# A time-mixing block cut into sixteen 256-token chunks and woven into the attention loop of a Perceiver layer

## The chip, the cores and the metric

The kernel runs on one core of one Trainium2 chip. The metric is the device time of one execution in microseconds. The core has five instruction streams that run side by side and meet only at semaphores: TensorE (PE, matmuls; its weight loads are shown as PEld), VectorE (DVE), ScalarE (ACT), GpSimd (POOL) and SyncE (SP, which here only issues DMAs).

## The reference

A layer over x (128 sequences of 32 tokens, 128 channels: 4096 tokens) and a context (128 x 257 x 96). Three blocks follow each other, each behind a layer norm with a residual; in a cut form:

```python
x = x + cross_attention(layernorm(x), ctx)        # 16 heads of 64, softmax over 257 context rows
x = x + time_mix(layernorm(x))                    # per sequence
x = x + ffn(layernorm(x))                         # each token through one of 8 experts (argmax)

# time_mix:
x_prev = x shifted by one token inside its sequence (zero first)
k, v = (x*mix_k + x_prev*(1-mix_k)) @ W_key.T, (x*mix_v + x_prev*(1-mix_v)) @ W_value.T
r = sigmoid((x*mix_r + x_prev*(1-mix_r)) @ W_receptance.T)
f_a = exp(k)*v / w**(t+1);  f_b = sum_of_head(exp(k)) / w**(t+1)       # w = exp(-exp(time_decay))
state_a, state_b = w**t * exclusive_cumsum(f_a), w**t * exclusive_cumsum(f_b)   # inf and nan become 0
wkv = (state_a + exp(time_first)*exp(k)*v) / max(state_b + exp(time_first)*sum_of_head(exp(k)), 1e-6)
out = (r * wkv) @ W_output.T
```

The shift and the running sums stay inside a sequence of 32 tokens, so the block can be cut at any sequence.

## The kernel before, in words

The tokens lie as 32 tiles ("groups", g) of 128 tokens, which are 4 sequences each. All tiles of x stay in SBUF in `R` (its first 128 columns are `X`), and each block adds its output there.

**Attention** is a software pipeline over the 128 sequences. One step handles one sequence in several stages at once, and each engine has its own copy of the step (`pe_step`, `act_step`, `dve_step`, `pool_step`). `where(it, j)` numbers them: an iteration of the hardware loop has eight steps, j = -1 to 6, and covers two groups. In a step, in this order:

- PE: transposes the context of sequence n+2 (`pe_ctxT`, L360), computes the scores of n+1 in tiles 0, 1 and 2 (`pe_scores`, L371), the queries of n+5 into bank 3 (`pe_q`, L383), and score tile 3, which uses bank 0 again and so waits for the exponential of tile 0 (`s_exp`). Then come probabilities times context (`pe_pv`, L394 and L400), once per group the output product (`pe_y`, L408, in steps 1 and 5), a small transpose that VectorE waits for (L449), and the transposes of the probabilities in two halves (`pe_probsT`, L416).
- DVE: copies the context (`cT`, L535), takes four row maxima (`nmax`, L511) with the low halves of Th between them (`Tl`, L507), then `ql` (L491), `rsum` (L518), `L12` (L522, printed as L), once per group the residual add (L526), and `Ol` (L530).
- ACT: `Th` (L462), four exponentials `Pe` (L468) with `qh` (L486) among them, and `Oh` (L477).
- POOL: `Pn` (L559, the probabilities times 1/sum, 128 x 1028), four small operations, and the split of the raw context in `chi` (L541) and `clo` (L545).

**Time mixing** follows in a pipeline of its own, `over_pairs`, over eight chunks (s) of 512 tokens. In a chunk DVE normalizes and clips, adds up and divides: `xn` (L656), `scl` (L1205), `sst` (L1209), `ekv` (L1216), `den` and `num` (L1219, L1221), `den` again (L1225), the reciprocal `rec` (L1228) and the running sums `cs` as one scan per sequence and sum (L1234, 32 per chunk). PE does five matmuls in fp32, ACT seven activations and POOL eight elementwise operations. Most tiles of this stage have two buffers.

**The expert block** follows: a third layer norm (`dve_var`, `dve_rstd`), routing, weight preparation and a loop over sorted tiles.

The order on each engine is the order of the code. Nothing is reordered by a scheduler, and an instruction that waits holds up all that stands behind it on its engine.

## Time and profile before

| | us |
|---|---|
| median of 3 runs (lowest, highest) | 1127.61 (1126.6, 1131.02) |
| the profiled execution's own time | 1121.37 |
| its span | 1119.7 |
| busy PE / DVE / ACT / POOL in the span | 921.9 / 856.5 / 665.6 / 634.8 |

The profile's page gives the busy time of each engine over the whole span, and the views behind it cut this by stretch. By the timeline the attention pipeline runs from about 43 us to 744 us, time mixing from there to 912 us, and the expert block to the end. Busy times are sums of instruction durations; PE's overlap, so that a PE that is busy all the time isn't by that alone at its limit, and successive instructions of DVE overlap by some 0.08 us.

### The profile page before, as it was taken

What the parts mean: (1) busy time and instruction counts of PE and PEld (TensorE: products, weight loads), DVE (VectorE), ACT (ScalarE), POOL (GpSimd) and SP (SyncE); (2) the same over time, 40 slices, a digit from 0 to 9 for tenths busy, and PEclk for the clock granted to TensorE, in tenths of its full rate; (3) what the DMA queues carried; (4) which work ended last, traced back from release to release, by engine and by line L of the source; (5) the groups of instructions that cost most, each with busy time, mean ns of one, the idle gap of its engine ahead of it and who ended that gap; (6) DMA issues with size and microseconds to landing.
All of it is one profiled execution on the core that took longest, in us unless ns stands there. A gap on an engine that the chain in (4) does not pass through costs nothing.

```text
span 1119.7 us, 30693 instructions
## 1 busy us (share of the span) xinstructions
PE 921.9 (82%) x9018; PEld 759.3 (68%) x9019; DVE 856.5 (76%) x2288; ACT 665.6 (59%) x1892; POOL 634.8 (57%) x983
## 2 busy tenths in 40 slices
PE   3899999999999999999999999965444436148885
PEld 3788888888888888888888888742222236136664
DVE  5888878878888887888888788757999976225543
ACT  2677767777776776777777677643121202136664
POOL 4466666665666666566566666626575510735453
PEclk9899999999999999999999999987676655659888
DMA  6100010010000001001000100039000000111110
GB/s 176 25 16 17 16 28 14 14 29 14 14 20 23 14 15 29 14 14 28 15 14 15 29 14 15 3 72 195 0 1 0 0 0 3 53 46 48 42 44 17
DMA packets 46488, 32.13 MB, mean 29 GB/s; under 512 B 6518, under 2 KB 44065, under 8 KB 46448
## 3 DMA queue, kind: packets, MB, share of 16 engines
q1 hardware_dynamic: 44144, 27.38, 10.0%
q0 software_dynamic: 2304, 4.25, 1.1%
q8 instruction: 20, 0.33, 0.1%
q14 instruction: 20, 0.16, 0.0%
HBM read 24.62 MB, written 7.52 MB: 29 GB/s over the span
## 4 chain that ended last, share of the span: by engine, by line
PE 72%; DVE 13%; issue 9%; ACT 3%; DMA 1%; POOL 1%; SPq 1%; ACTq 0%; DVEq 0%; POOLq 0%
PE bank L371 15%; PE bank L394 15%; PE bank L416 10%; PE bank L408 8%; PE bank L383 7%; DVE cs L1234 4%; PE bank L1114 4%; PE bank L1129 3%; PE bank L400 3%; PE bank L360 2%; DVE xn L656 1%; PE bank L663 1%; PE bank L1084 1%; DVE den L1225 1%; DMA wo_r<-in_L_xattn_Wo_dram 1%
## 5 line engine op out<-in xcount | busy, mean ns | idle before, releaser
L559 POOL TENSOR_TENSOR Pn<-Pe,rsum 128x1028 f32<-128x1028 f32 x128 | 243.1, 1899 | 226.6 <-DVE rsum L518 142.3
L468 ACT ACTIVATE Pe<-bank,nmax 128x257 f32<-128x257 f32 x512 | 239.5, 471 | 92.5 <-DVE nmax L511 92.4
L511 DVE TENSOR_REDUCE nmax<-bank 128x1 f32<-128x257 f32 x512 | 199.2, 409 | 1.2 <-PE bank L371 1.2
L371 PE MATMUL bank<-cT,qh 96*128 96x257 f16 x1024 | 185.2, 275 | 5.1 <-ACT Pe L468 4.1
L462 ACT ACTIVATE Th<-bank 128x512 f16<-128x512 f32 x256 | 138.9, 595 | 78.9 <-PE bank L416 78.9
L507 DVE TENSOR_TENSOR Tl<-bank,Th 128x512 f16<-128x512 f32 x256 | 172.8, 676 | 0.0
L371 PE MATMUL bank<-cT,ql 96*128 96x257 f16 x512 | 139.1, 272 | 0.0
L416 PE MATMUL bank<-identf,Pn 128*128 128x128 f32 x1024 | 133.5, 273 | 0.0
L416 PEld LDWEIGHTS bank<-identf,Pn 128*128 128x128 f32 x1024 | 109.8, 141 | 0.0
L491 DVE TENSOR_TENSOR ql<-bank,qh 96x512 f16<-96x512 f32 x128 | 87.9, 687 | 23.5 <-ACT qh L486 23.5
L468 ACT ACTIVATION_READ_ACCUMULATOR Pe<-bank,nmax 128x1 f32 x512 | 99.9, 195 | 0.0
L530 DVE TENSOR_TENSOR Ol<-bank,Oh 96x512 f16<-96x512 f32 x128 | 87.6, 685 | 12.4 <-ACT Oh L477 4.5
L371 PEld LDWEIGHTS bank<-cT,qh 96*128 96x128 f16 x1024 | 83.7, 97 | 18.8 <-issue 5.4
L383 PE MATMUL bank<-x1h,Ahi 128*96 (+1 forms) x512 | 93.5, 221 | 0.0
L383 PE MATMUL bank<-x1h,Alo 128*96 (+1 forms) x512 | 93.3, 220 | 0.0
L383 PE MATMUL bank<-x1l,Ahi 128*96 (+1 forms) x512 | 93.2, 220 | 0.0
L408 PE MATMUL bank<-Bhi,Oh 96*128 96x128 f16 x512 | 87.5, 219 | 1.5 <-DVE Ol L530 1.5
L408 PE MATMUL bank<-Bhi,Ol 96*128 96x128 f16 x512 | 87.4, 219 | 0.0
L408 PE MATMUL bank<-Blo,Oh 96*128 96x128 f16 x512 | 87.3, 219 | 0.0
L522 DVE COPY L<-bank 128x128 f16<-128x128 f16 x128 | 25.5, 200 | 73.1 <-PE bank L449 73.1
L477 ACT ACTIVATE Oh<-bank 96x512 f16<-96x512 f32 x128 | 75.8, 592 | 4.2 <-PE bank L400 3.2
L394 PE MATMUL bank<-Th,chi 128*96 128x512 f16 x256 | 76.6, 379 | 0.9 <-DVE Ol L530 0.9
(221 smaller groups left out, 2478.1 us busy)
## 6 DMA issues: line engine op xcount, KB each, us to landing
raw<-in_ctx_dram SPq DMA_DIRECT2D x32, 384.0 KB, 3.3
sorted_rows<-fill SPq DMA_DIRECT2D x1, 2620.0 KB, 20.8
xs<-sorted_rows SPq DMA_DIRECT2D x40, 65.5 KB, 1.8
R<-in_x_dram SPq DMA_DIRECT2D x4, 512.0 KB, 5.9
Z<-last_rows SPq DMA_DIRECT2D x128, 2.2 KB
w1r<-in_L_ffn_W_dram SPq DMA_DIRECT2D x8, 256.0 KB, 6.0
w2fr<-in_L_ffn_W_dram SPq DMA_DIRECT2D x8, 256.0 KB, 6.3
out_dram<-yout,idx POOLq DMA_INDIRECT x40, 2.3
```

The source lines that it names most:

```text
L371: last = nc.tensor.matmul(bank[SB[t]][:, 0:M], w[:, par, b, t * P:(t + 1) * P], cT[:, s4, c, 0:M], start=(k == 0), stop=(k == 2))
L383: last = nc.tensor.matmul(bank[b][0:CC, hh * P:(hh + 1) * P], w[:, h, :], a[:, tok], start=(k == 0), stop=(k == 2))
L394: nc.tensor.matmul(bank[6][0:CC, :], w[:, s8, c, :], p[:, par, c, :], start=(k == 0), stop=False)
L408: last = nc.tensor.matmul(bank[7][:, 512 - C:512], o[:, gp, h, :], w[:, h, :], start=(h == 0 and k == 0), stop=(h == H - 1 and k == 2))
L416: last = nc.tensor.transpose(bank[4 + c][:, t * P:(t + 1) * P], Pn[:, par, t, c * P:(c + 1) * P], identf[:, :])
L462: nc.scalar.activation(Th[:, n_par(j - 1), c, :], bank[4 + c][:, :], ACT.Copy).then_inc(s_Th, 1)
L468: nc.scalar.activation(Pe[:, n_par(j + 1), t, :], bank[SB[t]][:, 0:M], ACT.Exp, bias=nmax[:, n_par(j + 1), t:t + 1], accum_out=sums[:, n_p ...
L491: nc.vector.tensor_tensor(q_view(ql, par, c), bank[b][0:CC, :].rearrange("p (h b t) -> p h b t", h=QT, b=GB), q_view(qh, par, c), ALU.subt ...
L507: nc.vector.tensor_tensor(Tl[:, n_par(j - 1), t, :], bank[4 + t][:, :], Th[:, n_par(j - 1), t, :], ALU.subtract).then_inc(s_Tl, 1)
L511: nc.vector.tensor_reduce(nmax[:, n_par(j + 1), t:t + 1], bank[SB[t]][:, 0:M], AX.X, ALU.max, negate=True).then_inc(s_nmax, 1)
L530: nc.vector.tensor_tensor(Ol[sl], bank[6][0:CC, :].rearrange("p (h t) -> p h t", h=H), Oh[sl], ALU.subtract).then_inc(s_Ol, 1)
L559: nc.gpsimd.tensor_tensor(Pn[:, par, :, :], Pe[:, par, :, :], rsum[:, par, :].unsqueeze(2).broadcast_to([P, QT, M]), ALU.mult)\
```

## The change

The time-mixing block is cut into 16 chunks (c) of 256 tokens, two groups each. It no longer has a stage of its own: `pe_mix`, `act_mix`, `dve_mix` and `pool_mix` are called at the end of each step of the attention pipeline, and do the part of a chunk that the step number j names. Chunk c starts in iteration c+1, two iterations behind attention's start on its groups, and ends in iteration c+3. What is left after the last sequence is run down by `drain_mix`, in which the same steps go on without attention. The tiles of the stage have one buffer each and no longer share memory with attention's. The second layer norm's statistics are taken per group in the loop (bn_stats and bn_aggr on DVE), and its inverse root and the normalization are done on POOL (`pow` and a Newton step). The third layer norm's bn_stats are taken in the loop as well. The loads of the mixing weights, their transposes and the decay tables are needed ahead of the attention pipeline now. All of the block's matmuls go through bank 3, which `pe_q` also uses, so they stand at the end of a step, between the two halves of `pe_probsT`.

```diff
+    MG = 2
+    MT = MG * P
+    MCH = G // MG
...
                 wait(nc.tensor, s_pn, n + 1)
-                pe_probsT(n, n_par(j))
+                pe_probsT(n, n_par(j), 0)
+            pe_mix(it, j, n)
+            if exists(n):
+                pe_probsT(n, n_par(j), 1)
...
+            if j == 5 and chunk(it, 1) is not None:
+                c = it - 1
+                pe_mix_bank(it, j, n)
+                wait(nc.tensor, s_m["xc"], c + 1)
+                nc.tensor.matmul(bank[3][:, 0:MT], wka[:, :], xT33[:, :, 1:N + 1], start=True, stop=False)
+                nc.tensor.matmul(bank[3][:, 0:MT], wkb[:, :], xT33[:, :, 0:N], start=False, stop=True)\
+                    .then_inc(s_m["k"], 1)
...
+            if j == 5 and chunk(it, 1) is not None:
+                c = it - 1
+                wait(nc.scalar, s_m["ekv"], c)
+                wait(nc.scalar, s_m["k"], c + 1)
+                nc.scalar.activation(ek[:, :], bank[3][:, 0:MT], ACT.Exp).then_inc(s_m["ek"], 1)
+                wait(nc.scalar, s_m["xm"], 2 * c)
+                wait(nc.scalar, s_m["dx"], c + 1)
+                for k in range(2):
+                    last = nc.scalar.activation(mdx[:, k, :], dx[:, :], ACT.Copy, scale=mix[:, 1 + k:2 + k])
+                last.then_inc(s_m["mdx"], 1)
...
+            if j in (1, 2) and chunk(it, 2) is not None:
+                c, k = it - 2, j - 1
+                wait(nc.vector, s_m["st"], 2 * c)
+                wait(nc.vector, s_m["fab"], 2 * c + k + 1)
+                for b in range(MS):
+                    last = nc.vector.tensor_tensor_scan(cs[:, k, b, 1:N + 1], onesn[:, :], fab[:, k, b * N:(b + 1) * N],
+                                                        0.0, ALU.mult, ALU.add)
+                last.then_inc(s_m["cs"], 1)
...
+            if j == 3 and chunk(it, 2) is not None:
+                c = it - 2
+                wait(nc.vector, s_m["sst"], 2 * c)
+                for k in range(2):
+                    wait(nc.vector, s_m["st"], 2 * c + k + 1)
+                    nc.vector.tensor_scalar(scl[:, k, :], sraw[:, k, :], -FMAX, FMAX, ALU.max, ALU.min)\
+                        .then_inc(s_m["scl"], 1)
...
+            if j == 5 and chunk(it, 2) is not None:
+                c = it - 2
+                wait(nc.vector, s_m["o"], c)
+                wait(nc.vector, s_m["dm"], c + 1)
+                nc.vector.reciprocal(rec[:, :], denm[:, :]).then_inc(s_m["rec"], 1)
...
+        def drain_mix(step):
+            for j in range(2, 7):
+                step(LIT, j)
+            for j in range(-1, 7):
+                step(LIT + 1, j)
+            for j in range(-1, 3):
+                step(LIT + 2, j)
```

What `dve_mix` does in the other steps: j = -1 `ekv`; j = 1 the scans of the first sum and the residual add of chunk it-3; j = 2 two bn_stats of chunk it-3 and the scans of the second sum; j = 3 also `sst` twice; j = 4 `den`, `num`, `denm`. `pool_mix` does `fab` twice (j = 0), `sraw` (j = 1, 2), the normalization (j = 3, nine operations), `dx` (j = 5), `xm` twice and `oT` (j = 6). `pe_mix` has the transposes of xn (4), k (5), the head sums (6), v (-1), r (0) and the output (1). `act_mix` has the copy of xT (4), `ek` and `mdx` twice (5), `esum` (6), `er` and `er1` (0).

The order on VectorE from `rsum` to the first row maximum, in a step of the loop. Before:

```order
L518 RECIPROCAL rsum<-sums 128x4
L522 COPY L<-bank 128x128
L530 TENSOR_TENSOR Ol<-bank,Oh 96x16x32
L535 COPY cT<-bank 96x2x256
L23 REGISTER_ALU
L511 TENSOR_REDUCE nmax<-bank 128x1
```

The same place with the change, in step 4 (L is L12, er is er1):

```order
L638 RECIPROCAL rsum<-sums 128x4
L642 COPY L<-bank 128x128
L652 TENSOR_TENSOR Ol<-bank,Oh 96x16x32
L703 SCALAR_TENSOR_TENSOR den<-esum,nlw,sst 128x256
L706 SCALAR_TENSOR_TENSOR num<-ekv,nlw,sst 128x256
L711 SCALAR_TENSOR_TENSOR denm<-den,er 128x256
L721 COPY cT<-bank 96x2x256
```

Three operations with two SBUF tensors each now stand between `Ol` and the next step's `cT` and first maximum; in step 3 they are `scl` twice and `sst` twice.

The order on TensorE from the small transpose to the next step's context transposes. Before:

```order
L449 MATMUL bank<-ident,e12p 128x128 [waits s_elo,s_cT]
L416 MATMUL bank<-identf,Pn 128x128 [waits s_Tl,s_pn]
L416 MATMUL bank<-identf,Pn 128x128 x3
L416 MATMUL bank<-identf,Pn 128x128 [waits s_Tl]
L416 MATMUL bank<-identf,Pn 128x128 x3
L360 MATMUL bank<-ident,chi 96x128 [waits s_L12,s_cT,s_clo]
```

And now, in step -1:

```order
L465 MATMUL bank<-ident,e12p 128x128 [waits s_elo,s_cT]
L432 MATMUL bank<-identf,Pn 128x128 [waits s_Tl,s_pn]
L432 MATMUL bank<-identf,Pn 128x128 x3
L523 MATMUL bank<-xm,w2T 128x256 [waits m_xm,s_ql]
L432 MATMUL bank<-identf,Pn 128x128 [waits s_Tl]
L432 MATMUL bank<-identf,Pn 128x128 x3
L377 MATMUL bank<-ident,chi 96x128 [waits s_L12,s_cT,s_clo]
```

The mixing matmul stands between the halves of the probability transposes, and waits for `ql` of the same step as well as for its own input.

## Rows read from the trace of the kernel before

**Rows 1.** Busy us by stretch: PE, PEld, DVE, ACT, POOL, then PEclk and DMA.

```profile
110.00:440.00 330.00, 329.46 (x3592) 284.34 (x3590) 278.84 (x703) 248.59 (x734) 210.23 (x367) 1.00 0.07 18
800.00:900.00 100.00, 44.33 (x108) 24.32 (x108) 99.83 (x286) 19.17 (x32) 58.66 (x41) 0.66 0.00 0
```

**Rows 2.** Chain that ended last, two steps of attention: start, us, what.

```profile
399.96 2.68 PE bank L408 x48
402.64 0.06 PE bank L449
...
405.51 0.51 PE bank L371 x3
...
407.54 0.06 PE bank L449
...
412.26 0.06 PE bank L449
```

**Rows 3.** Timeline of all engines, score tile 3 of the first step.

```profile
404.89 0.48 ACT L468 ACTIVATE Pe<-bank,nmax 128x257 f32<-128x257 f32 x1 [0.63 <-DVE nmax L511]
...
405.50 0.11 PEld L371 LDWEIGHTS bank<-cT,qh 96*128 96x128 f16 x2 [0.18 <-ACT Pe L468]
```

**Rows 4.** Timeline of VectorE, 400 to 411 us.

```profile
402.74 0.23 DVE L522 COPY L<-bank 128x128 f16<-128x128 f16 x1 [2.31 <-PE bank L449]
...
407.83 0.16 DVE L518 RECIPROCAL rsum<-sums 128x4 f32<-128x4 f32 x1
...
408.20 0.69 DVE L530 TENSOR_TENSOR Ol<-bank,Oh 96x512 f16<-96x512 f32 x1
408.81 0.41 DVE L535 COPY cT<-bank 96x512 f16<-96x512 f16 x1
409.14 0.74 DVE L511 TENSOR_REDUCE nmax<-bank 128x1 f32<-128x257 f32 x2
```

**Rows 5.** Timeline of POOL in the same stretch.

```profile
400.58 1.90 POOL L559 TENSOR_TENSOR Pn<-Pe,rsum 128x1028 f32<-128x1028 f32 x1 [0.99 <-DVE rsum L518]
...
404.06 0.19 POOL L551 COPY cT<-c256T 96x2 f16 x1
408.16 1.90 POOL L559 TENSOR_TENSOR Pn<-Pe,rsum 128x1028 f32<-128x1028 f32 x1 [3.90 <-PE bank L416]
```

**Rows 6.** Timeline of VectorE in the time-mixing stage.

```profile
833.72 1.58 DVE L1225 SCALAR_TENSOR_TENSOR den<-den,er 128x512 f32<-128x512 f32 x1
...
882.03 1.49 DVE L1205 TENSOR_SCALAR scl<-sraw 128x512 f32<-128x512 f32 x2
...
899.34 0.76 DVE L1205 TENSOR_SCALAR scl<-sraw 128x512 f32<-128x512 f32 x2
...
902.66 0.68 DVE L1225 SCALAR_TENSOR_TENSOR den<-den,er 128x512 f32<-128x512 f32 x1
903.38 3.35 DVE L1228 RECIPROCAL rec<-den 128x512 f32<-128x512 f32 x1
```

**Rows 7.** Timeline of POOL in that stage.

```profile
833.21 1.55 POOL L828 TENSOR_TENSOR fab<-esum,iap 128x512 f32<-128x512 f32 x1
...
879.04 2.73 POOL L814 TENSOR_TENSOR sraw<-cs,apw 128x512 f32<-128x512 f32 x1 [1.62 <-DVE cs L1234]
```

**Rows 8.** Busy time of the scans of L1234 in one microsecond: DVE busy (instructions), PEclk.

```profile
893.80:894.80 1.00, 1.00 (x10) 0.50 0.00 0
```

**Rows 9.** Timeline of VectorE at both ends of the time-mixing stage.

```profile
744.03 0.29 DVE L526 TENSOR_TENSOR R<-R,bank 128x128 f32<-128x128 f32 x1 [3.02 <-PE bank L408]
...
912.08 0.22 DVE L630 TENSOR_TENSOR tmpv<-stats 128x32 f32<-128x32 f32 x1
```

**Rows 10.** Chain that ended last, a 512-wide fp32 matmul of the stage.

```profile
773.36 1.72 PE bank L1051 x2
```

**Rows 11.** Timeline of SyncE, the last issues ahead of the attention pipeline.

```profile
35.68 5.01 SPq L706 DMA_DIRECT2D dcy<-n_L_attn_time_first_dram  x8
```

**Rows 12.** Chain that ended last, TensorE's start into the attention pipeline.

```profile
43.63 0.41 PE bank L360 x4
```

More of the change, by code:

```diff
@@ L102, in perceiver_layer_kernel @@
         xn = sb("xn", [P, 2, CT, C])
+        stats2 = sb("stats2", [P, MG, 6])
+        mv = sb("mv", [P, MG, 2])
+        vep = sb("vep", [P, MG])
+        rs0 = sb("rs0", [P, MG])
+        rsq = sb("rsq", [P, MG])
+        rsv = sb("rsv", [P, MG])
+        rsc = sb("rsc", [P, MG])
+        rst2 = sb("rst2", [P, MG])
+        consts = sb("consts", [P, 3, MG])
+        xd = sb("xd", [P, MG, C])
+        xn2 = sb("xn2", [P, MG, C])
+        xT33 = sb("xT33", [P, MS, N + 1])
+        dx = sb("dx", [P, MT])
+        mdx = sb("mdx", [P, 2, MT])
+        xm = sb("xm", [P, 2, MT])
+        ek = sb("ek", [P, MT])
+        er = sb("er", [P, MT])
+        er1 = sb("er1", [P, MT])
+        esum = sb("esum", [P, MT])
+        ekv = sb("ekv", [P, MT])
+        fab = sb("fab", [P, 2, MT])
+        cs = sb("cs", [P, 2, MS, N + 1])
+        sraw = sb("sraw", [P, 2, MT])
+        scl = sb("scl", [P, 2, MT])
+        sst = sb("sst", [P, 2, MT])
+        num = sb("num", [P, MT])
+        den = sb("den", [P, MT])
+        denm = sb("denm", [P, MT])
+        rec = sb("rec", [P, MT])
+        oT = sb("oT", [P, MT])
         w2r = sb("w2r", [P, 4, C])
@@ L178, in perceiver_layer_kernel @@
         s_tdve = sem("s_tdve")
-        s_m = {n: sem("m_" + n) for n in ("w", "zero", "xn", "xT", "xc", "k", "v", "r", "ek", "er", "er1", "sum", "esum", "dx", "mdx", "xm",
-                                          "ekv", "fab", "cs", "st", "rec", "o", "y", "res", "ch")}
+        s_m = {n: sem("m_" + n) for n in ("w", "zero", "stat", "mv", "rs", "rs2", "xd", "xn", "xT", "xc", "k", "v", "r", "ek", "er", "er1", "sum",
+                                          "esum", "dx", "mdx", "xm", "ekv", "fab", "cs", "st", "scl", "sst", "dn", "num", "dm",
+                                          "rec", "o", "y", "res", "stat3")}
         s_w3 = sem("s_w3")
@@ L257, in lsb @@
             return late.enter_context(nc.sbuf_tensor(name, shape, dt))
-        xT33 = lsb("xT33", [P, 2, SEQ, N + 1])
-        dx = lsb("dx", [P, T])
-        mdx = lsb("mdx", [P, 2, T])
-        xm = lsb("xm", [P, 2, 2, T])
-        ek = lsb("ek", [P, 2, T])
-        er = lsb("er", [P, 2, T])
-        er1 = lsb("er1", [P, 2, T])
-        esum = lsb("esum", [P, 2, T])
-        ekv = lsb("ekv", [P, 2, T])
-        fab = lsb("fab", [P, 2, T])
-        cs = lsb("cs", [P, 2, SEQ, N + 1])
-        sraw = lsb("sraw", [P, 2, T])
-        scl = lsb("scl", [P, 2, T])
-        sst = lsb("sst", [P, 2, T])
-        num = lsb("num", [P, 2, T])
-        den = lsb("den", [P, T])
-        rec = lsb("rec", [P, 2, T])
-        oT = lsb("oT", [P, T])
         w1r = lsb("w1r", [P, E, FC, C])
@@ L576, in pipeline @@
+        LIT = B // 8
         def pipeline(eng, step):
-            for j in range(-1, 7):
-                step(0, j)
-            with eng.Fori(1, B // 8 - 1) as it:
+            for i in range(3):
+                for j in range(-1, 7):
+                    step(i, j)
+            with eng.Fori(3, LIT - 1) as it:
                 for j in range(-1, 7):
                     step(it, j)
-            for j in range(-1, 10):
-                step(B // 8 - 1, j)
+            for j in range(-1, 7):
+                step(LIT - 1, j)
+            for j in range(-1, 2):
+                step(LIT, j)
@@ L585, in time @@
+        def drain_mix(step):
+            for j in range(2, 7):
+                step(LIT, j)
+            for j in range(-1, 7):
+                step(LIT + 1, j)
+            for j in range(-1, 3):
+                step(LIT + 2, j)
         def time(a):
@@ L589, in over_seqs @@
         def over_seqs(a):
[L590 to L602 removed]
+            return a.unsqueeze(1).broadcast_to([P, MS, N])
         def over_tiles(eng, step, routed=True):
@@ L1238, in _ @@
-            over_pairs(dve_mix)(dve)
-            dve.wait_ge(s_m["res"], CH)
-            dve_var(chain, 2 * LS + 2)
-            dve_rstd(chain, 3)
             nc.vector.tensor_copy(R[:, :, C + 1], mean[:, :]).then_inc(s_row, 1)
```

430 lines of the change are left out of this document (233 added, 197 removed).

## The prediction

> **What bounds the kernel now.** I read the busy time by stretch first [rows 1]. Attention keeps PE busy for 329.46 of 330 us, but DVE is busy for 278.84 too, while time mixing, between 800 and 900 us, keeps DVE busy for 99.83 of 100 and PE for 44.33. So a stage limited by DVE is to be laid over one in which DVE has 15% left. Whether the left part can be used is a question of where it lies, and for that I read the chain and the timelines.
>
> The chain through attention lies on PE alone: an ordinary step takes 412.26 - 407.54 = 4.72 us, and the step behind a `pe_y` 407.54 - 402.64 = 4.90 [rows 2]. But DVE is just as close. Score tile 3 starts when ACT has finished the exponential of tile 0, which waited for DVE's first maximum [rows 3]. In the step behind `pe_y`, where DVE also has the residual add and a bn_stats, its first maximum comes late enough that tile 3 takes 0.51 us with its wait, where otherwise it follows gapless. From this I take that DVE has about 0.2 us of slack ahead of its first maximum in an ordinary step, and none in the step behind `pe_y`. Its only long idle time, 2.31 us, lies between `rsum` and `L12` in the step with `pe_y` [rows 4], because L449 stands behind the 2.68 us of L408 [rows 2]. The new work isn't put there: `dve_mix` comes behind `Ol`, ahead of `cT` and the first maximum.
>
> **What goes.** From the last residual add of attention to the third norm's first operation is 912.08 - 744.03 - 0.29 = 167.8 us [rows 9]. All of it goes, with the second norm and the tables in it.
>
> **What comes behind attention instead.** Chunk 15 can start only then, and runs alone. I add up its path: statistics 0.6; POOL's constant tables and the last `sraw`, which stand ahead of its normalization, 3; nine operations of normalization 2.9; transposes and copy 0.9; `dx`, `mdx`, `xm` 2.0; v and `ekv` 1.2; `fab` 0.6; scans 1.7; `sraw` 0.6; `scl`, `sst` 1.1; `den`, `num`, `denm` 1.0; `rec` 1.7; `oT` 0.7; output product, add and statistics 1.9, with some 0.1 us from engine to engine for 25 hops. This gives 22.5 us. I take the 512-wide durations at half and the short ones whole. Saved: 145.3 us.
>
> **Ahead of attention.** The loop now waits for the mixing weights. SP issues the last of them at 35.68 + 5.01 = 40.7 us [rows 11]; with 2 us to land, the transposes, a copy, two exponentials, a table load and five short operations of DVE in a row, PE starts at about 47.1 us instead of 43.6 [rows 12]: +3.5.
>
> **What comes into the loop.** DVE's durations: a two-input operation of 512 took 0.68 us alone [rows 6], so 0.34 for 256. Scans follow each other every 0.1 us, ten in 1 us [rows 8], so eight take 0.8. `rec` is half of 3.35 [rows 6], 1.67 us. Two `scl` took 0.76 [rows 6], so two of 256 take 0.4. bn_stats takes 0.2, and bn_aggr, which no row shows, lies between nothing and a bn_stats of 0.29; I take 0.2, since its input is tiny. PE: 1.72 us for 512 columns in fp32 at the lower level of 1.2 GHz [rows 10], so 0.43 for 256 at the granted 1.00 of the loop [rows 1]. PE comes to this point some 0.1 us before `ql` is done. So per step, before any contention, what arrives late ahead of the next first maximum is:
>
> - j = -1: PE 0.53; `ekv` is under it.
> - j = 0: no DVE work, but `er` and `er1` delay ACT by 0.87, of which 0.3 is slack: 0.57.
> - j = 1: scans and add, 1.1. j = 5: `rec`, and on ACT `mdx`, which waits for POOL's `dx`: 1.85.
> - j = 2: statistics, aggregate and scans 1.4, less 0.2: 1.2. j = 3: 1.07 - 0.2 = 0.87. j = 4: 1.0 - 0.2 = 0.8.
> - j = 6: PE 0.53.
>
> That is 7.4 us in an iteration. **Then there is POOL.** The operation that is `denm` now (L1225) took 1.58 us while POOL worked and 0.68 when it didn't, and two `scl` 1.49 and 0.76 [rows 6]. The times fit if one engine waits for the other's whole instruction: POOL's `fab` ran from 833.21 to 834.76, and L1225, started at 833.72, ended at 835.30, 0.54 us behind it [rows 6, 7]. In the loop `Pn` starts 408.16 - 407.83 = 0.33 us behind `rsum` and runs 1.90 [rows 4, 5], to 2.23. `Ol` ends 0.98 behind `rsum` (the start of `cT`) [rows 4]. So the two-input operations in steps 3 and 4 find POOL at work and wait 1.25 us; in step 2 the scans, which start 0.6 later, wait 0.66. In step 1 `pe_y` gives POOL time to finish all but `clo`: 0.3. Behind `Pn` come POOL's short operations, to 404.06 + 0.19 - 400.58 = 3.67 [rows 5]. For these I take 0.3 to 0.4 per step, as the run of scans held POOL's `sraw` out until it was over (2.73 us) [rows 7]. In step 3 POOL also has 2.9 us of normalization behind 3.67, more than the lengthened step leaves, so that `Pn` of step 4 starts some 0.4 late and the wait grows by as much, less the 0.15 already in reserve. Rounded: j = 1 1.45, j = 2 2.1, j = 3 2.5, j = 4 2.7, with the rest as above. The sum is 12.2 us per iteration.
>
> The Trainium skill ("SBUF — State Buffer", section "Who interferes with whom") says that VectorE's second read port is GpSimd's, that whoever issues first holds it for its whole instruction, and that a VectorE instruction with two SBUF inputs contends with GpSimd. The wait of L1225 agrees. By that rule the waiting `sraw` should have got its turn behind one scan, and it did not for 1.6 us. Held to strictly, it would put `e12p`, `chi` and `clo` in between as well and give the third rival's sum.
>
> **The sum.** Thirteen iterations with all parts: 13 x 12.2 = 158.6. Iteration 1 has only the front part: 2.7. Iteration 2 lacks the output part: 11.5. The last three steps: 2. Together 174.8. With 3.5 ahead and 145.3 saved it is +33 us on the profiled execution's own 1121.4, so 1154. The median of the runs shown lies 6 us above that execution, so I predict 1160 us.
>
> **Rivals.**
>
> - *POOL gives way.* The two-input operations of DVE get through, and POOL's own slack absorbs it: it has 1.0 us per step beyond its 3.67, and more where steps grow. For it: POOL is held out by scans [rows 7]. Against it: L1225, a single operation such as step 4 has [rows 6]. Then 7.4 us per iteration: 96.2 + 2.7 + 6.7 + 1.5 = 107, so 107 + 3.5 - 145.3 = -35, or 1093 us: faster. It decides from 9.9 us per iteration down, where the loop's cost equals what is saved.
> - *DVE's idle time takes it in.* If DVE may lag and catch up in the 2.31 us of each group, only PE's added work is left, 3.3 us per iteration: about 46 + 3.5 - 145.3 = -96, or 1032 us. Against it: the part of `pe_pv` ahead of `pe_y` waits for DVE's `Tl`, so the lag moves `pe_y` and the idle time with it.
> - *POOL's short operations come between as well*: 1.0 us more in each of the steps 2, 3 and 4, 15.2 us per iteration, 217 in all: 1203 us.
> - *PE's clock falls.* Steps 2 to 4 leave PE without work for 2 us and more at a stretch. In time mixing the granted clock was 0.66 on average, where PE was busy for 44% [rows 1]. If one step of an iteration ran at the lower level of 1.2 GHz, its 4.7 us of PE work would double: +4.7 x 13 = 61, 1221 us. Against it: PE stays busy for over 60% of each step.
>
> **Chances.** My forecast, 10.5 to 14 us per iteration, has 0.5 (its own range 1138 to 1184); POOL gives way 0.2; the idle time takes it in 0.05; the short operations come between 0.15; the clock 0.1. The likeliest case's lower end and the first rival's upper end meet near no change. The measurement can tell about 0.5% (6 us) from none. So slower by more than that 0.68, within it 0.07, faster 0.25. The range reaches from the first rival to the third, 1093 to 1203; what lies outside is the second, the fourth, and little of the others.
>
> **What the changed profile would show.** In attention, by stretch, PE well below 329 of 330 and DVE above 90% busy. An iteration of 55.6 us, where 8 steps now take 43.4. `denm` and the first `sst` and `scl` lasting over 1 us, with their ends at that of `Pn`; their shorter siblings at 0.42. An idle time of about 2.3 us ahead of `L12` in the steps with `pe_y` that has not shrunk. Score tile 3 waiting for ACT's exponential by 2 us in steps 3 to 5. The last attention add to the third norm in 22 us. A granted clock near 1.00 in the loop. The prediction is wrong if `denm` shows 0.4 us, if the idle time is gone, or if POOL's `pow` on 128 x 2 takes microseconds, for then PE's transposes in step 4 wait for `xn`.

## The result and the profile after

The changed kernel takes 1174.0 us, the median of four runs (1170.0 to 1177.3), against 1127.1 us for the kernel before on the same chip (1121.3 to 1131.0): a ratio of 1.042, with a 95% interval from 1.036 to 1.048. It is slower by 47 us. The profiled execution took 1177.3 us with a span of 1175.6, so it lies 3.3 us above its median, where that of before lay 5.7 below its own. The prediction was 1160 us.

Line numbers have moved: `L12` is L642 now, `rsum` L638, `Pn` L745, score tiles L388, and TensorE's transposes of `xn` are L505. The busy time by stretch, in the columns of [rows 1]:

```profile
110.00:440.00 330.00, 292.63 (x2928) 243.77 (x2927) 270.15 (x705) 214.02 (x622) 217.37 (x390) 0.97 0.05 15
440.00:760.00 320.00, 277.30 (x2810) 231.93 (x2809) 269.58 (x705) 201.77 (x587) 209.73 (x370) 0.98 0.05 15
...
938.00:965.00 27.00, 8.07 (x21) 4.22 (x20) 15.67 (x58) 4.29 (x10) 12.01 (x30) 0.57 1.07 200
```

PE has fallen from 329.46 of 330 us [rows 1] to 292.63, and VectorE has not risen: 270.15 against 278.84. No engine is full now. So the loop must be held up by waits between engines, which no sum of busy times shows.

The 55.9 us between the spans (1175.6 and 1119.7) are made up so. Each is read from a timeline: TensorE's start into the pipeline (its second `ctxT`; a first one runs 2.0 us earlier before, 6.3 us earlier now), the last residual add of attention, the first operation of the third norm.

| part | before, us | after, us | difference | predicted |
|---|---|---|---|---|
| start to TensorE's second `ctxT` | 43.63 | 55.38 | +11.75 | +3.5 |
| from there to the end of the last add | 700.7 | 882.8 | +182.1 | +174.8 |
| from there to the third norm | 167.8 | 30.0 | -137.7 | -145.3 |
| the rest | 207.6 | 207.4 | -0.2 | 0 |

An iteration, from one start of `L12` to the eighth after it, takes 55.53 us on average where it took 43.34. The length of a step j below is the time from the `L12` of step j to the next one. The steps 3 and 4 of iteration 7 show what is in an iteration. VectorE's timeline:

```profile
457.31 0.16 DVE L638 RECIPROCAL rsum<-sums 128x4 f32<-128x4 f32 x1
...
457.67 0.69 DVE L652 TENSOR_TENSOR Ol<-bank,Oh 96x512 f16<-96x512 f32 x1
458.28 1.52 DVE L691 TENSOR_SCALAR scl<-sraw 128x256 f32<-128x256 f32 x2
459.72 0.75 DVE L696 SCALAR_TENSOR_TENSOR sst<-sraw,scl 128x256 f32<-128x256 f32 x2
...
464.12 0.16 DVE L638 RECIPROCAL rsum<-sums 128x4 f32<-128x4 f32 x1
...
465.09 2.14 DVE L703 SCALAR_TENSOR_TENSOR den<-esum,nlw,sst 128x256 f32<-128x256 f32 x1
467.15 0.47 DVE L706 SCALAR_TENSOR_TENSOR num<-ekv,nlw,sst 128x256 f32<-128x256 f32 x1
467.55 0.41 DVE L711 SCALAR_TENSOR_TENSOR denm<-den,er 128x256 f32<-128x256 f32 x1
...
474.08 0.23 DVE L642 COPY L<-bank 128x128 f16<-128x128 f16 x1 [2.31 <-PE bank L465]
...
961.86 0.49 DVE L703 SCALAR_TENSOR_TENSOR den<-esum,nlw,sst 128x256 f32<-128x256 f32 x1
```

GpSimd (POOL) in the same stretch:

```profile
457.55 1.90 POOL L745 TENSOR_TENSOR Pn<-Pe,rsum 128x1028 f32<-128x1028 f32 x1 [2.56 <-DVE rsum L638]
...
461.55 0.19 POOL L770 TENSOR_TENSOR vep<-mv,consts 128x2 f32<-128x2 f32 x1
...
464.30 0.61 POOL L786 TENSOR_TENSOR xn<-xd,rst 128x256 f32<-128x256 f32 x1
464.87 2.08 POOL L745 TENSOR_TENSOR Pn<-Pe,rsum 128x1028 f32<-128x1028 f32 x1
```

And where TensorE stood still, from its timeline:

```profile
461.80 0.40 PE L388 MATMUL bank<-cT,qh 96*128 96x257 f16 x2 [1.96 <-ACT Pe L553]
...
465.06 0.41 PE L505 MATMUL bank<-identf,xn 128*128 128x128 f32 x2 [0.73 <-POOL xn L786]
...
469.28 0.40 PE L388 MATMUL bank<-cT,qh 96*128 96x257 f16 x2 [1.48 <-ACT Pe L553]
```

Two things are to be seen. `den` lasts 2.14 us and ends 0.28 behind the end of `Pn` (464.87 + 2.08), where it takes 0.49 when nothing runs on GpSimd (961.86 us, behind the loop); the idle time ahead of `L12` is still 2.31 us, as in [rows 4]. That is what the prediction described. `num` and `denm` behind it keep their 0.47 and 0.41 us in all iterations, beside `e12p` of GpSimd. The other was not in its sum: TensorE waits for `xn`, the last of nine operations that GpSimd begins only behind `Pn`, `e12p`, `chi` and `clo`. From the start of `Pn` to the end of `xn` this chain takes 7.4 us (457.55 to 464.91). The wait is short here, because VectorE is late too. The experiments turn on it.

### The profile page after: what moved, and what is told of

Same layout as the page of the kernel before. It is cut to its first block, busy times and chain, and to the rows that moved or that the text cites. A ratio compares the mean times of both kernels' runs of the same rounds, so it can differ in the third digit from the quotient of the medians.

```text
span 1175.6 us, 31270 instructions
## 1 busy us (share of the span) xinstructions
PE 948.5 (81%) x9098; PEld 785.3 (67%) x9099; DVE 866.3 (74%) x2356; ACT 677.1 (58%) x1945; POOL 691.3 (59%) x1194
## 4 chain that ended last, share of the span: by engine, by line
PE 42%; POOL 23%; issue 17%; DVE 8%; ACT 5%; POOLq 1%; DMA 1%; SPq 1%; ACTq 0%; DVEq 0%
POOL Pn L745 9%; PE bank L411 8%; PE bank L388 7%; PE bank L425 4%; PE bank L432 4%; PE bank L1264 4%; PE bank L400 3%; POOL chi L727 2%; PE bank L1279 2%; POOL sorted_rows L1068 2%; DVE nmax L631 2%; ACT Pe L553 2%; PE bank L417 1%; DVE cs L677 1%; POOL e12p L752 1%
## 5 line engine op out<-in xcount | busy, mean ns | idle before, releaser
L745 POOL TENSOR_TENSOR Pn<-Pe,rsum 128x1028 f32<-128x1028 f32 x128 | 245.2, 1915 | 265.1 <-DVE rsum L638 183.6
L388 PE MATMUL bank<-cT,qh 96*128 96x257 f16 x1024 | 188.4, 279 | 96.0 <-ACT Pe L553 94.8
L547 ACT ACTIVATE Th<-bank 128x512 f16<-128x512 f32 x256 | 141.6, 593 | 54.6 <-PE bank L432 53.2
L388 PEld LDWEIGHTS bank<-cT,qh 96*128 96x128 f16 x1024 | 85.4, 98 | 118.9 <-ACT Pe L553 87.4
L432 PE MATMUL bank<-identf,Pn 128*128 128x128 f32 x1024 | 151.6, 278 | 0.0
L388 PE MATMUL bank<-cT,ql 96*128 96x257 f16 x512 | 140.9, 275 | 0.0
L432 PEld LDWEIGHTS bank<-identf,Pn 128*128 128x128 f32 x1024 | 118.3, 145 | 5.9
L652 DVE TENSOR_TENSOR Ol<-bank,Oh 96x512 f16<-96x512 f32 x128 | 87.7, 685 | 22.5 <-ACT Oh L562 19.1
L642 DVE COPY L<-bank 128x128 f16<-128x128 f16 x128 | 26.0, 203 | 86.3 <-PE bank L465 86.0
L411 PE MATMUL bank<-Tl,chi 128*96 128x512 f16 x256 | 79.9, 395 | 0.0
```

The source lines that it names most:

```text
L388: last = nc.tensor.matmul(bank[SB[t]][:, 0:M], w[:, par, b, t * P:(t + 1) * P], cT[:, s4, c, 0:M], start=(k == 0), stop=(k == 2))
L411: nc.tensor.matmul(bank[6][0:CC, :], w[:, s8, c, :], p[:, par, c, :], start=(k == 0), stop=False)
L432: last = nc.tensor.transpose(bank[4 + c][:, t * P:(t + 1) * P], Pn[:, par, t, c * P:(c + 1) * P], identf[:, :])
L547: nc.scalar.activation(Th[:, n_par(j - 1), c, :], bank[4 + c][:, :], ACT.Copy).then_inc(s_Th, 1)
L652: nc.vector.tensor_tensor(Ol[sl], bank[6][0:CC, :].rearrange("p (h t) -> p h t", h=H), Oh[sl], ALU.subtract).then_inc(s_Ol, 1)
L745: nc.gpsimd.tensor_tensor(Pn[:, par, :, :], Pe[:, par, :, :], rsum[:, par, :].unsqueeze(2).broadcast_to([P, QT, M]), ALU.mult)\
```

## The experiments

All times are medians; the kernel before lay between 1127.4 and 1129.2 us on each occasion, with single runs from 1120.6 to 1136.2. "Iteration" is the mean of iterations 3 to 14, between starts of `L12`.

**1. The wait for `Pn` taken away.** In the steps 2, 3 and 4, VectorE's mixing work is called ahead of `rsum` instead of behind `Ol`.

```
+            if j in (2, 3, 4):
+                dve_mix(it, j)
             if exists(n + 1):
                 wait(nc.vector, s_exp, QT * (n + 2))
...
-            dve_mix(it, j)
+            if j not in (2, 3, 4):
+                dve_mix(it, j)
```

> Against the changed kernel (1174 us) one thing is moved: in steps 2, 3 and 4 VectorE's mixing work stands ahead of rsum of the same step, where GpSimd has finished its short operations, and no longer behind Ol, where Pn runs. The same instructions, the same order among themselves. Theory (the wait for Pn is what makes these steps long): in the changed kernel den took 1.97 us on average against 0.52 alone, the pair of scl 1.1 to 1.5 against 0.5 to 0.8, the second run of scans 1.95 against 1.03; together 3.0 to 3.4 us per iteration. They are gone, den is near 0.5, and the time is 1174 - 14 x 3.2 = 1129 us (1122 to 1137). Rival 1 (a two-input operation of VectorE is long wherever it stands while GpSimd is busy, or the steps are long for another reason): den stays above 1 us, 1174. Rival 2: rsum, and Pn behind it, are now later by the mixing work, and TensorE waits for Pn: the step is no shorter, 1170 to 1190.

Measured: 1175.7 us, an iteration 56.15. Nothing was gained, though the waits of the first kind are gone: `den` takes 0.47 us in every iteration where it took 1.97 on average, the pair of `scl` 0.48 for 1.03, the second run of scans 1.02 for 1.95. Step 2 fell from 7.54 to 5.76 us and step 3 from 6.54 to 5.73, but step 1 rose from 6.31 to 7.63 (a part of this is only moved: work ahead of the `L12` of step 2 counts to step 1) and step 4 from 9.76 to 11.73. The second rival was right in that nothing would be gained, but TensorE does not wait for `Pn`. TensorE's waits between 110 and 880 us, of the changed kernel and of this one:

```profile
PE bank L388 <- ACT Pe L553: 83.8, 67, 2.2
PE bank L505 <- POOL xn L786: 9.8, 12, 2.3
```

```profile
PE bank L505 <- POOL xn L789: 43.8, 14, 3.6
PE bank L377 <- DVE L L644: 24.3, 26, 1.1
PE bank L388 <- ACT Pe L553: 17.6, 28, 0.9
```

The columns are us in total, times, longest. Waiting for ScalarE's exponentials, which is VectorE's lateness passed on, fell from 83.8 to 17.6 us, and waiting for GpSimd's `xn` rose from 9.8 to 43.8: 3.1 us in each iteration. The 24.3 us at L377 are new as well: they are for `L12`, which now comes behind the mixing work. And in step 4 the place ahead of `rsum` is not free of GpSimd, whose `pow` (`rs`) runs there:

```profile
456.17 0.47 DVE L706 SCALAR_TENSOR_TENSOR den<-esum,nlw,sst 128x256 f32<-128x256 f32 x1
```

```profile
456.17 1.02 POOL L777 TENSOR_TENSOR rs<-vep,consts 128x2 f32<-128x2 f32 x1
```

Here it is GpSimd that is held up: `rs` takes 1.02 to 1.78 us in this run and 0.70 in the changed kernel.

**2. The sizes cut, the places kept.** `scl`, `sst`, `den`, `num`, `denm` work on one column, and the scans of step 2 too, so most of the second operand of the mixing is left out.

```
-                nc.vector.scalar_tensor_tensor(num[:, :], ekv[:, :], nlw[:, 1:2], sst[:, 0, :], ALU.mult, ALU.add)\
+                nc.vector.scalar_tensor_tensor(num[:, 0:1], ekv[:, 0:1], nlw[:, 1:2], sst[:, 0, 0:1], ALU.mult, ALU.add)\
```

> Against the changed kernel the sizes are cut and every place is kept: scl, sst, den, num, denm work on 1 of 256 columns, and each scan of step 2 on 1 of 32, so most of the second operand of the mixing is left out (the buffers are set once at the start). Theory (VectorE waits until GpSimd's whole Pn is over): the first operation behind Ol in steps 3 and 4 still ends with Pn, den still lasts over 1.2 us, and only the sizes are saved, some 0.25 us for each of seven operations and little for the scans: 2 us per iteration, 1174 - 14 x 2 = 1146 us (1135 to 1156). Rival (the two engines share a rate, and an operation is slowed in proportion to its size): den is near 0.2 us, and the 3.2 us of contention go as well, 1174 - 14 x 5.2 = 1101 us.

Measured: 1141.7 us, inside the range, and an iteration of 53.28: 2.25 us saved in each. VectorE and GpSimd in a step 4:

```profile
342.69 0.41 DVE L703 SCALAR_TENSOR_TENSOR den<-esum,nlw,sst 128x1 f32<-128x1 f32 x1
343.02 1.94 DVE L706 SCALAR_TENSOR_TENSOR num<-ekv,nlw,sst 128x1 f32<-128x1 f32 x1
344.88 0.14 DVE L711 SCALAR_TENSOR_TENSOR denm<-den,er 128x1 f32<-128x1 f32 x1
```

```profile
342.47 0.61 POOL L786 TENSOR_TENSOR xn<-xd,rst 128x256 f32<-128x256 f32 x1
343.04 1.90 POOL L745 TENSOR_TENSOR Pn<-Pe,rsum 128x1028 f32<-128x1028 f32 x1
```

An operation on one column takes 1.94 us and ends 0.02 behind `Pn`; its neighbour of the same size takes 0.14. (`den` ends with `xn` in the same way.) So for an operation with two SBUF inputs the size does not matter: it waits for the whole of GpSimd's instruction. The Trainium skill ("SBUF — State Buffer", "Who interferes with whom") calls the shared port pair an exclusive lock under which the other engine "**fully blocks** (not throttle)"; these rows agree with it.

For `scl`, which reads one SBUF tensor, the size does matter. On one column the pair runs through beside a `Pn`, where on 256 columns it took 1.52 us (458.28 above):

```profile
336.09 1.90 POOL L745 TENSOR_TENSOR Pn<-Pe,rsum 128x1028 f32<-128x1028 f32 x1 [1.97 <-DVE rsum L638]
```

```profile
336.82 0.20 DVE L691 TENSOR_SCALAR scl<-sraw 128x1 f32<-128x1 f32 x2
```

**3. The idle time filled.** Both runs of scans stand ahead of `rsum` in step 1; `scl` to `denm` stand ahead of `rsum` in step 5. There VectorE has its 2.3 us of idle time behind `rsum`, and GpSimd has nothing to do.

```
+            dve_mix_early(it, j)
             if exists(n + 1):
                 wait(nc.vector, s_exp, QT * (n + 2))
...
-            if j in (1, 2) and chunk(it, 2) is not None:
-                c, k = it - 2, j - 1
...
+        def dve_mix_early(it, j):
+            if j == 1 and chunk(it, 2) is not None:
...
+                for k in range(2):
+                    wait(nc.vector, s_m["fab"], 2 * c + k + 1)
...
-            if j == 3 and chunk(it, 2) is not None:
+            if j == 5 and chunk(it, 2) is not None:
...
-            if j == 4 and chunk(it, 2) is not None:
+            if j == 5 and chunk(it, 2) is not None:
```

> VectorE's idle time of 2.3 to 2.6 us in the two steps with pe_y is filled: both runs of scans stand ahead of rsum in step 1, and scl, sst, den, num, denm ahead of rsum in step 5; rec stays behind Ol in step 5. Nothing is left out. Theory: the steps 2, 3 and 4 lose what the mixing added there except statistics (2.85 + 1.81 + 2.68 - 0.3 = 7.0 us), step 1 loses its 0.95 of scans, the idle time takes 1.9 and 2.25 us and is nearly gone, and GpSimd's normalization in the shorter step 3 gives back some 0.5: 7.4 us per iteration, 1174 - 13.5 x 7.4 = 1074 us (1062 to 1092). Rival 1 (rsum, Pn and L12 later move the whole step with them, as the prediction said of a lag of VectorE): the 4.15 us come back in the steps 1 and 5, 1174 - 13.5 x 3.3 = 1129 us. Rival 2 (GpSimd, which has 6.6 us of work in step 3, becomes the bound): Pn of step 4 holds TensorE by 2 us, about 1100.

Measured: 1162.6 us, an iteration 55.22, where 1074 us was expected: of 100 us, 11 were gained. The steps 1, 2 and 3 did as expected (5.66, 5.21, 4.70), but step 4 took 11.36 and step 5 9.23. TensorE's two long waits in iteration 7:

```profile
451.25 0.41 PE L505 MATMUL bank<-identf,xn 128*128 128x128 f32 x2 [2.50 <-POOL xn L790]
...
465.51 0.40 PE L388 MATMUL bank<-cT,qh 96*128 96x257 f16 x2 [3.28 <-ACT Pe L553]
```

The first is the one known by now. The second is ScalarE's, from its waits:

```profile
ACT mdx L581 <- POOL dx L796: 30.3, 13, 2.7
```

`mdx` waits for GpSimd's `dx`, which stands behind a `Pn` that comes later now, and behind `mdx` on ScalarE stand `Th` and the next exponentials. What follows such a stop costs as well: TensorE runs on at a lower clock. The busy times and, third from the end, the granted clock from 466 us on:

```profile
466.00:468.00 2.00, 2.00 (x9) 1.06 (x7) 1.26 (x4) 1.29 (x5) 0.28 (x1) 0.62 0.00 0
468.00:470.00 2.00, 2.00 (x12) 1.78 (x11) 1.00 (x3) 0.59 (x1) 1.84 (x3) 0.53 0.00 0
```

That is near the lower of the two levels (1.2 GHz is 0.5), behind 3.28 us of standing still; from 470 us on it is 1.00 again.

**4. The same with VectorE's share nearly gone.** The scans, `scl` to `denm` and `rec` on one column each, in the places of experiment 3; their work is left out.

```
-                nc.vector.reciprocal(rec[:, :], denm[:, :]).then_inc(s_m["rec"], 1)
+                nc.vector.reciprocal(rec[:, 0:1], denm[:, 0:1]).then_inc(s_m["rec"], 1)
```

> The places of the run before (idle time filled), and the scans, scl, sst, den, num, denm and rec on one column each, so that nearly all of VectorE's mixing work is left out (R, ekv and the statistics remain), while TensorE, ScalarE and GpSimd do all of theirs. Theory: what stays is the work of TensorE, 3.3 us per iteration as worked out in the prediction, with ScalarE's two exponentials inside it: 1174 - 13.5 x 8.9 = 1054 us (1046 to 1068). Rival (ScalarE's and GpSimd's added work, or more waits between the engines, set a floor of their own, as the waits on L465 hint): 1075 us or more, over 5 us per iteration.

Measured: 1126.8 us, an iteration 53.14, so 9.8 us more than before the change with hardly any mixing work on VectorE. The rival came true. L505 waited 36.6 us in 15 times. What my prediction had charged to VectorE was, in these places, a floor that GpSimd and ScalarE set as well; experiment 8 gets below it with all of the work done.

**5 and 6. GpSimd's chain shortened, without and with the move of experiment 1.** The seven small operations of the normalization, `vep` to `rst`, go to the end of step 2; `xd` and `xn` stand ahead of `pool_prep` in step 3.

```
+            pool_norm(it, j)
             if exists(n + 4):
                 if (j + 4) % GB == 0:
...
+        def pool_norm(it, j):
+            if j == 3 and chunk(it, 1) is not None:
...
         def pool_mix(it, j):
-            if j == 3 and chunk(it, 1) is not None:
...
+            if j == 2 and chunk(it, 1) is not None:
+                c = it - 1
+                wait(nc.gpsimd, s_m["mv"], MG * (c + 1))
```

> The changed kernel with one move on GpSimd alone: the seven small operations of the normalization (vep to rst) go from step 3 to the end of step 2, and xd and xn in step 3 stand ahead of the preparation of the next context rows instead of behind it. New theory after the first four runs: TensorE's transposes of xn in step 4 (L505) wait for a chain on GpSimd, Pn, e12p, chi, clo and then nine operations, 6.6 us, and this second chain is nearly as long as VectorE's wait for Pn. In the changed kernel it shows as only 9.8 us of waiting at L505 in the loop, since VectorE is late as well. So taking it away alone gives little: 9.8 + 14 x 0.35 us (Pn of step 4, and with it den, earlier), 1174 - 12 = 1162 us (1157 to 1168). Rival (VectorE is the only limit of the changed kernel): 1174. Rival 2 (GpSimd's chain is the limit and VectorE's wait only rides on it): 1135 or less.

> The first run (VectorE's mixing work of steps 2 to 4 ahead of rsum, 1175.7 us) with the same move on GpSimd. Theory of two chains side by side: there the wait for Pn was gone but L505 waited 43.8 us in 14 steps for xn, 3.1 us in each, so that nothing was gained. With both gone step 4 falls from 11.73 to about 8.4 us, and the time is 1175.7 - 14 x 3.2 = 1131 us (1122 to 1142). Rival (the place ahead of rsum is bad in itself, since Pn and L12 come later by the mixing work): the wait goes from L505 to L377 or L465, 1160 or more.

Measured: 1162.3 and 1125.4 us, both inside their ranges. With the changed kernel and experiment 1 they make a square:

| | GpSimd's chain long | chain shortened |
|---|---|---|
| VectorE behind `Ol` | 1174.0 us, iteration 55.53 | 1162.3 us, 54.88 |
| VectorE ahead of `rsum` | 1175.7 us, 56.15 | 1125.4 us, 52.40 |

Either alone is worth 12 us or nothing; both together are worth 49. Two chains of nearly one length lay side by side. In experiment 6, L505 waits 5.2 us in all between 110 and 880 us, and the largest wait is that for `L12` at L377, 37.1 us in 39 times. In experiment 8, where the work stands ahead of `rsum` in the idle time, it is gone.

**7 and 8. The idle time filled, with the other two waits mended.** Experiment 7 is experiment 3 with `dx` at the end of step 4. Experiment 8 adds the move of experiment 5 and both `sraw` in step 1.

```
-            if j == 5 and chunk(it, 1) is not None:
+            if j == 4 and chunk(it, 1) is not None:
                 c = it - 1
                 wait(nc.gpsimd, s_m["mdx"], c)
...
-            if j in (1, 2) and chunk(it, 2) is not None:
-                c, k = it - 2, j - 1
+            if j == 1 and chunk(it, 2) is not None:
+                c = it - 2
                 wait(nc.gpsimd, s_m["sst"], 2 * c)
```

> The third run (idle time filled, 1162.6 us) with one move: GpSimd's dx goes from step 5 to the end of step 4. There ScalarE waited 30.3 us in 13 steps for dx ahead of mdx, and behind mdx stand Th and the exponentials, for which TensorE waited up to 3.3 us in step 6. Theory: this in-order wait is why filling the idle time gained so little in step 5 (9.23 us instead of 6.6): 1162.6 - 13 x 2.6 = 1129 us (1122 to 1140); mdx no longer waits. Rival (rec and the later rsum make step 5 long): 1155 to 1163.

> The idle time filled, dx early, the small operations of the normalization in step 2 with xd and xn ahead of the preparation, and both sraw of GpSimd in step 1, where it has time. Nothing is left out. Theory: besides dx (2.6 us) the 34.5 us of waiting at L505 go as well, step 4 falls from 11.4 to about 8, and an iteration is 55.2 - 2.6 - 3.2 = 49.4 us: 1162.6 - 13.5 x 5.8 = 1084 us (1074 to 1100), faster than the kernel before. Rival (GpSimd, with 3.67 + 2.2 us in step 2 and 3.67 + 1.2 in step 3, holds Pn back): 1105 to 1130.

Measured: 1114.5 us (ratio to before 0.986, interval 0.982 to 0.990) and 1067.9 us (0.947, 0.943 to 0.951), iterations of 51.51 and 48.69. Both lie below their ranges. The gain of `dx` alone is larger than I expected, 48 us against 33. Step 5 fell by the expected 2.6 us, to 6.63, but step 4 fell by 0.7 as well and step 6 by 0.4, 13 times 3.7 in all. The granted clock of the loop's first stretch rose from 0.96 to 0.98 with it; how much of the 1.1 us is the clock's I have not separated. In experiment 8, TensorE's waits in the loop (110 to 820 us) and the busy time of the first stretch:

```profile
PE bank L388 <- ACT Pe L553: 16.9, 34, 1.4
PE bank L377 <- POOL clo L735: 2.0, 13, 0.2
```

```profile
110.00:440.00 330.00, 321.72 (x3296) 269.82 (x3295) 292.92 (x808) 242.15 (x707) 238.89 (x439) 1.00 0.06 17
```

L505 is gone from the list. TensorE is busy for 321.72 of 330 us, VectorE for 292.92, and the clock is 1.00. Nothing was removed from the work. What the normalization and the two `sraw` give apart was not measured.

**9. The tables taken off the path ahead of attention.** From experiment 8: TensorE's transposes of `w2r` in step 3 of iteration 0, ScalarE's part in its steps 3 and 5, VectorE's in 4 and 6.

```
+            if at(it, j, 0, 3):
+                pe_mix_bank(it, j, n)
+                nc.tensor.wait_ge(s_w2, 16 * (7 + 2 * HS))
+                for a in range(4):
+                    last = nc.tensor.transpose(bank[3][:, a * P:(a + 1) * P], w2r[:, a, :], identf[:, :])
+                last.then_inc(s_w2T, 1)
...
-            dve_tables()
             pipeline(nc.vector, dve_step)
```

> The best run (1067.9 us) with the mixing weights and tables taken out of the path ahead of attention: TensorE's transposes of w2r stand in step 3 of iteration 0, ScalarE's copy and exponentials in its steps 3 and 5, VectorE's short operations in its steps 4 and 6; the first use is in iteration 1. Theory: TensorE no longer stands still for 3.9 us ahead of the loop, nor falls to the lower clock behind it (the first steps took 3.5 us more), and the moved work costs some 1.5 us inside iteration 0: 1067.9 - 3.6 - 3.5 + 1.5 = 1062 us (1058 to 1066). Rival (the in-order waits inside iteration 0 cost as much as they did ahead of it): 1068.

Measured: 1064.3 us (0.941, 0.937 to 0.945), the lowest median of a version that does all the work. It lies 3.5 us below experiment 8, where I expected 5.9, but the intervals overlap, so that the gain isn't shown by the times. TensorE's start, here and, as it was, in experiment 1:

```profile
48.43 0.28 PE L377 MATMUL bank<-ident,chi 128*96 128x128 f16 x2 [1.61 <-DVE cT L761]
```

```profile
42.81 0.63 PE L1213 MATMUL bank<-identf,w2r 128*128 128x128 f32 x4 [1.38 <-DVE ql L609]
47.37 0.42 PE L377 MATMUL bank<-ident,chi 128*96 128x128 f16 x2 [3.93 <-issue]
```

The two starts can't be compared, since the matmuls ahead of them ran at different speeds in the two executions (shown below). But the stop of 3.93 us is gone, and from this start to the first `L12` it takes 7.5 us, as in the kernel before. On the other side iteration 0 grew by 2.2 us (38.80 against 36.59 from the first `L12` to the eighth), and each later iteration by 0.1.

**10. The price of `rec`.** Experiment 9 with the edit to `rec` of experiment 4 alone: the reciprocal is left out but for one column.

> The run before with rec on 1 of 256 columns, so that the reciprocal of the mixing's denominator is left out (the rest of the buffer is set once at the start). Price of rec by itself: in step 5 both TensorE's k (0.86 us) and VectorE's rec (1.67 us) are new, and the step is 1.45 us longer than it was. If k and rec lie side by side and rec is the longer, about 0.6 to 0.9 us per iteration come back: 1062 - 14 x 0.8 = 1051 us. Rival, the prediction's step, by which the 1.85 us of step 5 are rec's and mdx's alone: 1062 - 14 x 1.45 = 1042 us. Rival 2 (k alone makes the step): 1060.

Measured: 1060.3 us, an iteration 48.40 against 48.79, with an interval that overlaps that of experiment 9. Step 5 fell from 6.63 to 6.15 us. So with `k` beside it on TensorE the longest operation of VectorE is worth 0.4 us per iteration by the trace, between the theory's 0.8 and the second rival's nothing, and not the 1.45 of the prediction's step.

**11. The place alone, with GpSimd's chains relieved.** Experiment 9 with `scl` and `sst` back in step 3 and `den`, `num`, `denm` back in step 4, behind `Ol`.

```
+            if j == 3 and chunk(it, 2) is not None:
...
+            if j == 4 and chunk(it, 2) is not None:
...
         def dve_mix_early(it, j):
             if j == 1 and chunk(it, 2) is not None:
...
-            if j == 5 and chunk(it, 2) is not None:
```

> The first kernel of this call with scl and sst back in step 3 and den, num and denm back in step 4, behind Ol as in the changed kernel; the scans stay in the idle time, and GpSimd's chains stay relieved. Theory: this is the price of the place alone when nothing on GpSimd hides it: the operations' own 2.3 us less 0.4 of slack, and the wait for Pn twice, 1.25 us less what the operations in front of them take: 3.2 us per iteration, 1062 + 14 x 3.2 = 1107 us (1098 to 1115), with den or num again over 1.2 us and ending with Pn. Rival (the place costs only the operations' own time): 1062 + 14 x 1.9 = 1089 us. Rival 2 (the gain of the best run came from GpSimd's order alone): 1062 to 1068.

Measured: 1129.5 us, an iteration 53.18: the place costs 4.4 us per iteration and 65 us in all, where I expected 3.2 and 45. It ended above my range. `den` waits less than expected, 0.47 to 1.46 us, but in step 3 the pair of `scl` meets the whole of `Pn`, which starts later than it did: GpSimd's small operations of the normalization now stand ahead of it, to 429.00 us. So a part of the 4.4 us comes from this place together with GpSimd's order:

```profile
428.90 2.19 DVE L720 TENSOR_SCALAR scl<-sraw 128x256 f32<-128x256 f32 x2
```

```profile
428.95 1.99 POOL L785 TENSOR_TENSOR Pn<-Pe,rsum 128x1028 f32<-128x1028 f32 x1
```

## Why the prediction was right in its time and wrong in its reasons

I predicted 1160 us and the median is 1174.0. The profiled execution took 1177.3 us where the sum gave 1154: some 8 us more ahead of attention, 7 in the loop, 8 behind it. 9 us of this difference are only where the two profiled executions lie in their spreads.

**The loop.** The forecast of 12.2 us per iteration met 12.19. That it met so closely is luck. Against the steps one by one:

| j | -1 | 0 | 1 | 2 | 3 | 4 | 5 | 6 |
|---|---|---|---|---|---|---|---|---|
| predicted | 0.53 | 0.57 | 1.45 | 2.1 | 2.5 | 2.7 | 1.85 | 0.53 |
| measured | 0.67 | 0.94 | 1.13 | 2.85 | 1.81 | 2.68 | 1.45 | 0.64 |

Single steps are off by up to 0.75 us, one way and the other, and the errors cancel. The wait for `Pn` is there, and `den` bears it as the first operation behind `Ol`, not `denm`: 1.97 us on average against 0.47 in experiment 1. With the scans of step 2 (1.95 against 1.02 us) and `scl` (1.03 against 0.48) it adds some 3.0 us to an iteration, where I had charged 4.8 to contention. The difference of 1.8 us came back elsewhere: some 0.6 of it is the wait for `xn` (9.8 us at L505, 2.3 of them in iteration 1), and the rest I have not assigned.

**The step that failed** is the one on step 3 and the work of GpSimd: "In step 3 POOL also has 2.9 us of normalization behind 3.67, more than the lengthened step leaves, so that `Pn` of step 4 starts some 0.4 late". I followed that chain to `Pn` and not to its other reader. TensorE's transposes in step 4 wait for `xn`, and on TensorE the second half of `probsT`, `ctxT` and the next scores stand behind them. I named that wait only for the case that `pow` takes microseconds; it takes 0.70, and the wait comes all the same. Nor is the normalization 2.9 us long: `vep` to `xn` takes 3.4. Iteration 1 shows the wait bare, since there the front part of a chunk runs with none of VectorE's work: I forecast +2.7 us and it took +7.2, of which step 4 alone took 11.53 us where it takes 7.08 without a chunk. With the chain shortened (experiment 5) the same step takes 7.65. TensorE in this step:

```profile
132.65 0.49 PE L505 MATMUL bank<-identf,xn 128*128 128x128 f32 x2 [2.26 <-POOL xn L786]
```

The granted clock of 132 to 134 us is 0.71, that of 134 to 136 us 0.50, so that the loss is larger than the wait. In the other iterations the wait is mostly covered by VectorE's lateness, and that is why the sum could come out: it held one of two parallel chains, and the other was not much longer.

**What follows for the rivals.** "POOL gives way" is refuted by experiment 2. Its price is refuted with it: with the wait for `Pn` gone, 7.4 us per iteration were to be left, and 12.8 were (experiment 1), or 9.1 with GpSimd's chain shortened too (experiment 6). "POOL's short operations come between as well" is refuted by `num` and `denm`, which waited for none of them in the changed kernel. "DVE's idle time takes it in" got a chance of 0.05, with the reason that the lag would move `pe_y` and the idle time along. For work behind `Ol` that holds, as the 2.31 us ahead of `L12` show. For work ahead of `rsum` in the same two steps it does not: experiment 8 gets 48.69 us per iteration. So the reason was one of place, and I had taken it for one of the schedule. "PE's clock falls" did not come true for the changed kernel, whose loop runs at 0.97 and 0.98, but it adds to the price of a long stop in iteration 1 and in experiments 1 and 3.

**Ahead of attention** I forecast +3.5 us and the profiled execution shows +11.75. In experiment 1, whose program is the same up to the loop, TensorE starts at 47.37 us, +3.7. So the term was right, and the other 8.0 us come from the execution and not from the program. TensorE's timeline of the changed kernel, then of experiment 1:

```profile
21.44 2.02 PE L1190 MATMUL bank<-wkT,wqT 64*128 64x96 f32 x8 [0.37 <-ACT wvT L1098]
...
50.82 0.63 PE L1210 MATMUL bank<-identf,w2r 128*128 128x128 f32 x4 [1.38 <-DVE ql L609]
55.38 0.42 PE L377 MATMUL bank<-ident,chi 128*96 128x128 f16 x2 [3.93 <-issue]
```

```profile
21.31 1.13 PE L1193 MATMUL bank<-wkT,wqT 64*128 64x96 f32 x8 [0.47 <-ACT wvT L1101]
```

The same eight matmuls take 2.02 us in one execution and 1.13 in the other. Such groups stay at 2.02 us until 42 us in the changed kernel's, and at 1.11 to 1.15, but for one, in that of experiment 1. Why, no run shows. What I did miss is what comes behind the stop: the granted clock is 0.50 from 56 to 64 us, and from the second `ctxT` to the first `L12` it takes 10.7 us instead of 7.5, a loss of 3.2 that stands in the loop's 182.1. With the 4.5 us of iteration 1 these are 7.7 us, and the loop is over by 7.3.

**Behind attention** 30.0 us instead of 22.5. TensorE and VectorE there:

```profile
946.73 0.66 PE L505 MATMUL bank<-identf,xn 128*128 128x128 f32 x2 [6.23 <-POOL xn L786]
948.14 1.19 PE L511 MATMUL bank<-xT,wka 128*128 128x256 f32 x2 [0.75 <-ACT xT L572]
...
952.86 1.19 PE L523 MATMUL bank<-xm,w2T 128*128 128x256 f32 x2 [0.75 <-ACT esum L588]
```

```profile
954.19 0.42 DVE L671 TENSOR_TENSOR ekv<-ek,bank 128x256 f32<-128x256 f32 x1 [6.77 <-PE bank L523]
...
958.02 0.42 DVE L684 TENSOR_TENSOR R<-R,bank 128x256 f32<-128x256 f32 x1 [1.14 <-PE bank L534]
...
958.88 1.02 DVE L677 TENSOR_TENSOR_SCAN cs<-onesn,fab 128x32 f32<-128x32 f32 x8
...
968.18 0.21 DVE L879 TENSOR_TENSOR tmpv<-stats 128x32 f32<-128x32 f32 x1
```

I summed the data's path, transposes, `dx`, `mdx`, `xm`, v. TensorE's order puts `k`, `ek` and the block sum ahead of v, 4.7 us from L511 to L523, and the clock is low there (0.57 by the window above): from the end of `xT` to that of `ekv` it takes 6.7 us, where I had 3.2. It is the same error again, on VectorE too: the second run of scans starts 2.0 us behind the end of the first (955.50 + 1.39), since the residual add of chunk 14 and its statistics stand ahead of it, and the add waits for TensorE (L534). `xn` was late as well, 8.4 us behind attention's last add instead of 6.5. Together that is the failed part of this term.

**By the signs I had given:** the iteration, the 2.3 us ahead of `L12` and the waits of score tile 3 (1.96 and 1.48 us above) were right. `denm` at 0.41 us was one of my signs of being wrong; what it showed was only that `den`, the first of the three, bears the wait. The first `sst` hardly ever waited, since the pair of `scl` ahead of it had, and the way to the third norm took 30 us instead of 22. VectorE over 90% busy was wrong, at 82%, and that was the sign that the waits were not all VectorE's.
